# A fused attention and feed-forward layer on one core: the head's products ordered term by term, and six steps in other places

## The chip, the cores and the metric

The kernel runs on one core of a Trainium2 chip. The metric is the device time of one execution in microseconds (us), and a lower time is better. The core's engines have names that are used below: PE is TensorE (matrix products), DVE is VectorE, ACT is ScalarE, POOL is GpSimd, and SP is SyncE, which issues nearly all of the transfers. Each engine works through its own program in order and waits for the others on semaphores.

## The reference

A layer of a network is applied to `x`, 2 sequences of 2048 rows with 1024 features:

```python
qkv = einsum('bsc,cf->bsf', layernorm(x), Wqkv) + bqkv      # q, k, v of 256 features
attn = softmax(q @ k.T * scale, axis=-1)                    # 4 batches by a reshape, d = 256
x = x + (attn @ v) @ Wo + bo
h = relu(layernorm(x) @ up_w) ** 2                          # 2048 wide
shared = h @ down_w
routed = (layernorm(x) @ fc1_w @ expert_w) * sum(top2(gate)) @ fc2_w
x = x + layernorm2(shared + routed) * gamma + beta
```

All of it is in float32.

## The kernel before

**Products.** Each operand of a product is kept as a rounded high half and a low half, which is the operand minus its high half. A product of two operands is three matmuls that add into one bank of PSUM: high by high, high by low, low by high (`mm3`, L2182 to L2184). ACT mostly makes the high half, and DVE (L1191) or POOL (L1960) makes the low half by a subtraction. The names end in `h` and `l`.

**Stages.** The program has four stages, and each engine has its part of all four, written out by hand in one order.

1. *Head.* `e2`, the product of `expert_w` (`et`) and `fc2_w` (`f2`), is accumulated over k = 0 to 3 into seven banks (`lt` 0 to 3, halves `hh` 0 and 1). The eighth, (3,1), is multiplied at the end, since its bank first holds the sums of the first layernorm. Meanwhile DVE takes the statistics of the rows of chunk 0 (`BATCH_NORM`). PE sums them over partitions by two small products, `combine1a` (L2200) and `combine1b` (L2205). DVE then works out mean and root (L1235 to L1266), and the 16 row groups are normalised, those in `NORM_DVE` on DVE (L1273) and the others on ACT (L1017).
2. *Chunks.* In each of 8 chunks of rows the normalised rows `xi` are turned into `xt` (L1285), split into `xh` and `xl` by `slab_hi` and `slab_low`, and multiplied with `w` for q, k and v. DVE takes the statistics of the next chunk and forms sums of feed-forward weights on the way (`pb`, L1300 to L1313). The low half that each chunk needs first is `slab_low(c + 1, 0)`. It is made during chunk c, between the low halves of v.
3. *Attention.* There are 16 pairs of strips, with scores (`kh`, `q`), the row maximum on DVE, the exponential on ACT (`prob`, L937), a transpose, low halves of `pt`, the product with v, and the product with `Wo`. POOL adds the folded bias `bob` to `x` (`xadd`, L2015), DVE adds the attention output (`residual`, L1364) and takes the statistics (`ln2`, L1380 on, with nm at L1386), and POOL normalises (`norm2`, L2006). The folded bias itself is `bv` times `Wo`, four float32 matmuls (L2297) whose result DVE adds to `bo` (L1710).
4. *Feed-forward.* There are four blocks n of 1024 rows. Each has 70 slots of up products and 70 (in the last block 60) of down products. A slot is 12 matmuls, fed by weights that ACT and POOL split (`w_low`: wr0l, wr1l, wr2l) and operands from `x_low`. The function `turnover` starts a slot on an engine. `add_beta` (L2051) adds beta to the residual rows on POOL.

What the change touches: the order of PE's products and sums in the head, the tables `NORM_DVE` and of ACT's staging, `slab_low` on DVE, the place of the bias on PE and DVE, the order of POOL's `xadd` and `norm2` in pairs 7 and 14/15, `ln2(14)`, `x_low(0, 6, ·)`, and the last two calls of `add_beta`.

## Time and profile before

| | before |
|---|---|
| median of 3 runs | 2357.73 us (2353.16 to 2359.95) |
| the profiled execution | 2362.06 us |
| its span | 2360.1 us |
| mean granted clock of PE | 0.996 |
| PE busy | 2310.1 us, 98% of the span |
| DVE busy | 1760.5 us, 75% |
| POOL busy | 1568.0 us, 66% |
| ACT busy | 906.1 us, 38% |

The span is the time from the first to the last instruction in the profile; it differs from the execution's own time by 2.0 us. Busy times are of one execution. In a timeline the bracket behind a row says how long the engine stood idle before it, and which instruction of which engine ended that.

### The profile page before, as it was taken

Reading aid. Unit: us, or ns where it says so; the run is one execution under the profiler, and the core shown is the slowest. Engines: PE = TensorE matmul, PEld = TensorE weight load, DVE = VectorE, ACT = ScalarE, POOL = GpSimd, SP = SyncE. Lnnn points to the kernel's source line nnn. Section 1 sums busy time; section 2 is a strip of 40 time slices with the busy share of each in tenths; the row PEclk is TensorE's granted clock in tenths of the full one; section 3 lists DMA queues with packets and bytes.
Section 4 is the critical chain, followed back from the end, with each engine's and each line's share of the span. In section 5 each row is a group of like instructions: output and inputs, shape, how many; then the busy total and the mean of one; then the engine's idle time right before and its main releaser. Section 6 shows DMA issues by size and latency. Waiting matters only on the chain.

```text
span 2360.1 us, 31294 instructions
## 1 busy us (share of the span) xinstructions
PE 2310.1 (98%) x11224; PEld 1925.1 (82%) x11224; DVE 1760.5 (75%) x2952; ACT 906.1 (38%) x1705; POOL 1568.0 (66%) x1175
## 2 busy tenths in 40 slices
PE   8999999999999999999999999999999999999998
PEld 6888888888888788878887887888887788777786
DVE  5999868778787735854689765579895468979968
ACT  4322243333333344444432443442344443244452
POOL 5556626665665776699567479847649974866762
PEclk9999999999999999999999999999999999999999
DMA  7889656778768633543335345435534433544342
GB/s 260 296 308 317 220 161 187 208 237 297 213 197 234 208 103 94 130 125 115 99 129 180 94 130 126 120 94 161 151 109 122 132 108 112 178 148 129 91 141 86
DMA packets 200137, 386.47 MB, mean 164 GB/s; under 512 B 19120, under 2 KB 78640, under 8 KB 198192
## 3 DMA queue, kind: packets, MB, share of 16 engines
q1 hardware_dynamic: 198832, 382.38, 53.6%
q8 instruction: 90, 1.47, 0.3%
q10 hardware_dynamic: 1152, 2.10, 0.2%
q14 instruction: 63, 0.52, 0.1%
HBM read 260.67 MB, written 90.18 MB: 149 GB/s over the span
## 4 chain that ended last, share of the span: by engine, by line
PE 59%; DVE 15%; POOL 12%; issue 5%; DMA 5%; SPq 2%; ACT 1%; DVEq 0%; POOLq 0%; ACTq 0%
PE ps L2182 20%; PE ps L2184 19%; PE ps L2183 19%; POOL hq L2044 4%; DVE pturn L1337 2%; POOL wr1l L1960 2%; POOL wr2l L1960 2%; POOL wr0l L1960 2%; DMA pland<-pturn 2%; DVE xr L1608 1%; DMA stf<-ups 1%; POOL xr L2051 1%; DVE hq L1517 1%; SPq L640 1%; DVE mx L1320 1%
## 5 line engine op out<-in xcount | busy, mean ns | idle before, releaser
L1960 POOL TENSOR_TENSOR wr2l<-stf,wr2h 128x512 fp32r<-128x512 f32 x183 | 258.6, 1413 | 145.4 <-ACT wr2h L969 145.2
L1960 POOL TENSOR_TENSOR wr1l<-stf,wr1h 128x512 fp32r<-128x512 f32 x183 | 262.5, 1435 | 139.2 <-ACT wr1h L969 139.2
L1960 POOL TENSOR_TENSOR wr0l<-stf,wr0h 128x512 fp32r<-128x512 f32 x184 | 260.7, 1417 | 141.9 <-ACT wr0h L969 141.8
L969 ACT CAST wr0h<-stf 128x512 fp32r<-128x512 f32 x184 | 114.4, 622 | 300.4 <-PE ps L2184 247.9
L969 ACT CAST wr1h<-stf 128x512 fp32r<-128x512 f32 x183 | 113.8, 622 | 299.6 <-PE ps L2184 246.1
L969 ACT CAST wr2h<-stf 128x512 fp32r<-128x512 f32 x183 | 113.9, 622 | 299.1 <-PE ps L2184 244.9
L1960 POOL TENSOR_TENSOR pt<-pland,pt 128x512 fp32r<-128x512 f32 x120 | 153.6, 1317 | 78.7 <-ACT pt L947 78.7
L937 ACT ACTIVATE prob<-ps,nm 128x512 f32<-128x512 f32 x128 | 86.3, 687 | 247.6 <-DVE nm L1328 247.6
L1337 DVE STREAM_TRANSPOSE pturn<-prob 128x512 f32<-128x512 f32 x128 | 131.9, 1089 | 54.0 <-DMA pland<-pturn 51.5
L1191 DVE TENSOR_TENSOR hr1l<-hq,hr1h 128x512 fp32r<-128x512 f32 x78 | 98.7, 1265 | 88.1 <-ACT hr1h L988 88.0
L1191 DVE TENSOR_TENSOR hr2l<-hq,hr2h 128x512 fp32r<-128x512 f32 x78 | 98.1, 1258 | 87.3 <-ACT hr2h L988 87.3
L1191 DVE TENSOR_TENSOR hr0l<-hq,hr0h 128x512 fp32r<-128x512 f32 x78 | 96.0, 1231 | 87.3 <-ACT hr0h L988 87.3
L2182 PE MATMUL ps<-pt,vh 128*128 128x256 f32 x512 | 145.8, 285 | 5.3 <-DVE pt L1191 5.2
L2183 PE MATMUL ps<-pt,vh 128*128 128x256 f32 x512 | 145.6, 284 | 0.0
L2184 PE MATMUL ps<-pt,vl 128*128 128x256 f32 x512 | 145.5, 284 | 0.0
L2044 POOL TENSOR_TENSOR hq<-hq,hq 128x512 f32<-128x512 f32 x90 | 140.6, 1562 | 0.0
L1960 POOL TENSOR_TENSOR xl<-xt,xh 128x512 fp32r<-128x512 f32 x54 | 71.9, 1343 | 72.2 <-ACT xh L927 72.1
L2006 POOL TENSOR_SCALAR x<-x,nm,rst 128x1024 f32<-128x1024 f32 x28 | 33.6, 1211 | 119.8 <-DVE rst L1205 119.8
L2182 PE MATMUL ps<-xh,wh 128*128 128x512 f32 x256 | 102.1, 399 | 3.6 <-DVE xl L1191 3.6
L2182 PEld LDWEIGHTS ps<-pt,vh 128*128 128x128 f32 x512 | 98.9, 193 | 7.2 <-issue 6.0
L2182 PE MATMUL ps<-kh,q 128*128 128x512 f32 x256 | 101.1, 395 | 2.7 <-ACT prob L937 2.7
L2183 PE MATMUL ps<-kl,q 128*128 128x512 f32 x256 | 100.5, 393 | 0.0
(490 smaller groups left out, 7746.5 us busy)
## 6 DMA issues: line engine op xcount, KB each, us to landing
stf<-ups SPq DMA_DIRECT2D x160, 256.0 KB, 3.2
stf<-downs SPq DMA_DIRECT2D x160, 256.0 KB, 2.9
pland<-pturn SPq DMA_DIRECT2D x120, 256.0 KB, 4.7
stf<-in_upw_dram SPq DMA_DIRECT2D x120, 256.0 KB, 2.7
stf<-in_down_dram SPq DMA_DIRECT2D x88, 256.0 KB, 2.7
x<-in_x_dram SPq DMA_DIRECT2D x32, 512.0 KB, 6.6
x1d<-x SPq DMA_DIRECT2D x32, 512.0 KB, 5.7
xi<-in_xc_dram SPq DMA_DIRECT2D x7, 2048.0 KB, 9.0
```

Source lines behind the costliest of these rows:

```text
L640: eng.dma_start(land(g)[:, 512 * i + 32 * n * h:512 * i + 32 * n * (h + 1)], turned(g)[32 * i:32 * i + 32, :].rearrange("p (k s) -> p k s" ...
L937: eng.activation(prob[:, 512 * kb:512 * kb + 512], ps[:, kb, :], ACT.Exp, bias=nm[:, 0:1], scale=1.0 / 16, accum_out=rs[:, kb:kb + 1]).the ...
L969: eng.copy(hi, src).then_inc(*a_w.up(K))
L1191: eng.tensor_tensor(lo, src, hi.bitcast(F32), ALU.subtract).then_inc(*done)
L1320: eng.reduce_max(mx[:, kb:kb + 1], ps[:, kb, :], AX.X).then_inc(*v_mx.up((g, kb)))
L1337: eng.transpose(turned(g)[:, :].rearrange("p (k s b) -> p s k b", k=4, b=32)[:, 4 * kb:4 * kb + 4], prob[:, 512 * kb:512 * kb + 512].rearr ...
L1960: eng.tensor_tensor(lo, src, hi.bitcast(F32), ALU.subtract).then_inc(*done)
L2006: eng.tensor_scalar(x2n[C][i][:, :], x1t[i][:, :], nm2[:, i:i + 1], rst2[:, i:i + 1], ALU.add, ALU.mult).then_inc(*g_x2.up(g))
L2044: eng.tensor_tensor(hq[o][:, c, :], hq[a][:, c, :], hq[b][:, c, :], op).then_inc(*g_hs.up((n, name, c)))
L2182: eng.matmul(o, ah, bh, start=first, stop=False)
L2183: eng.matmul(o, ah, bl, start=False, stop=False)
L2184: return eng.matmul(o, al, bh, start=False, stop=last)
```

## The change

**Head.** For k = 2 and 3 PE multiplies one term over all banks before the next term (`e2_term`). The first sum of statistics stands after 8 of these matmuls and the second after 7 more. `NORM_DVE` has ten groups in place of six. POOL makes the low half of `et` 3 ahead of that of `f2` 3. ACT splits `w` (2,0) before it normalises, takes out `e2` banks for `lt` 0 ahead of `slab_hi(0, 0)`, and splits `w` (1,1) before those for `lt` 1.

**Chunks.** `slab_low(c + 1, 0)` stands ahead of the turns of slabs 2 and 3.

**Folded bias.** Its four matmuls move from between chunk 7's v and the scores of strip 1 to between the scores of strips 2 and 3, and DVE's addition moves with them, to after the first low halves of `pt`.

**Pair 7.** POOL's `xadd(6, 0)` stands ahead of `norm2(5)`.

**Pairs 14 and 15.** `ln2(14)` works on one column at a time (two by turns), and its root has other steps (22 small instructions in place of 11 after the aggregate). POOL's `norm2(14)` comes ahead of `xadd(15)`, whose halves move into slots 0 and 1, and SP stores both results in slot 0.

**Feed-forward.** `x_low(0, 6, ·)` goes one slot later; the last betas go from slots 50 and 53 of up to slots 33 and 37 of down.

```diff
-        NORM_DVE = (1, 3, 6, 9, 12, 15)
+        NORM_DVE = (1, 3, 5, 7, 8, 9, 11, 12, 14, 15)
...
-            for k in STG[:12]:
+            for k in STG[:13]:
                 stage_hi(k)
             norm_rows(0, [g for g in range(16) if g not in NORM_DVE])
-            stage_hi(STG[12])
+            e2_evac(0)
             slab_hi(0, 0)
-            e2_evac(0)
+            stage_hi(STG[13])
+            e2_evac(1)
             slab_hi(0, 1)
-            e2_evac(1)
-            for k in STG[13:15]:
-                stage_hi(k)
+            stage_hi(STG[14])
...
                     low(v_parts(c, t), a_v[c, t], v_v.up((c, t)))
+                    if c < 7 and t == 1:
+                        slab_low(c + 1, 0)
                     if c < 7 and t < 2:
                         turn1(c + 1, 2 * t)
                         turn1(c + 1, 2 * t + 1)
-                    if c < 7 and t == 1:
-                        slab_low(c + 1, 0)
...
-            ln2(14, *range(15))
+            ln2(14)
...
                 if C == 7:
+                    xadd(C - 1, 0)
                     norm2(C - 2, 0)
                     norm2(C - 2, 1)
-                if C < 15 and C != 8:
+                    xadd(C - 1, 1)
+                elif C < 15 and C != 8:
                     xadd(C - 1)
...
-            xadd(15)
+            norm2(14, 0)
+            norm2(14, 1)
...
-                        if s in (1, 2):
-                            norm2(14, s - 1)
+                        if s < 2:
+                            xadd(15, s)
...
-                        if fin and s in (50, 53):
-                            add_beta(n, (s - 50) // 3, xrl[(s - 50) // 3])
...
+                        if s in (33, 37):
+                            add_beta(n, s // 37, xrl[s // 37])
...
+            e2_term(2, eth, f2h, 0)
+            w.wait_ge(*stg_lo(("et", 2)))
+            e2_term(2, etl, f2h, 0)
+            combine1a(0)
+            w.wait_ge(*stg_lo(("f2", 2, 0)))
+            e2_term(2, eth, f2l, 0)
+            w.wait_ge(*a_stg["f2", 2, 1])
+            e2_term(2, eth, f2h, 1)
+            combine1b(0)
...
                     scores(even)
                     if C >= 2:
                         outputs(C - 2)
+                    else:
+                        folded_bias()
                     scores(odd)
```

How the rows move on PE in the head, at k = 2, where `mv,quad` is `combine1a` and `dm,quad` is `combine1b`. Before:

```order
L2223 MATMUL ps<-f2h,eth 128x512 x4
L2223 MATMUL ps<-f2h,etl 128x512 x4
L2223 MATMUL ps<-f2l,eth 128x512 x4
L2200 MATMUL ps<-mv_54,quad 128x32
L2182 MATMUL ps<-f2h,eth 128x512
L2183 MATMUL ps<-f2l,eth 128x512
L2184 MATMUL ps<-f2h,etl 128x512
L2182 MATMUL ps<-f2h,eth 128x512
L2183 MATMUL ps<-f2l,eth 128x512
L2184 MATMUL ps<-f2h,etl 128x512
L2182 MATMUL ps<-f2h,eth 128x512
L2183 MATMUL ps<-f2l,eth 128x512
L2184 MATMUL ps<-f2h,etl 128x512
L2205 MATMUL ps<-dm_55,quad 128x16
```

After:

```order
L2260 MATMUL ps<-f2h,eth 128x512 x4
L2260 MATMUL ps<-f2h,etl 128x512 x4
L2235 MATMUL ps<-mv_54,quad 128x32
L2260 MATMUL ps<-f2l,eth 128x512 x4
L2260 MATMUL ps<-f2h,eth 128x512 x3
L2240 MATMUL ps<-dm_55,quad 128x16
L2260 MATMUL ps<-f2h,etl 128x512 x3
L2260 MATMUL ps<-f2l,eth 128x512 x3
L2260 MATMUL ps<-f2h,eth 128x512 x7
L2260 MATMUL ps<-f2h,etl 128x512 x7
```

The first sum stands four matmuls earlier and the second, counted from it, two.

How they move on DVE between chunks 0 and 1, where `xt<-xi` is a turn, `xl<-xt,xh` the chunk's first low half and `vl` a low half of v. Before:

```order
L1285 STREAM_TRANSPOSE xt_98<-xi_97 128x512
L1285 STREAM_TRANSPOSE xt_99<-xi_97 128x512
L1191 TENSOR_TENSOR vl<-ps,vh 128x2x128
L1285 STREAM_TRANSPOSE xt_100<-xi_97 128x512
L1285 STREAM_TRANSPOSE xt_101<-xi_97 128x512
L1191 TENSOR_TENSOR xl<-xt_98,xh 128x512
L1191 TENSOR_TENSOR vl<-ps,vh 128x2x128 x2
```

After:

```order
L1286 STREAM_TRANSPOSE xt_98<-xi_97 128x512
L1286 STREAM_TRANSPOSE xt_99<-xi_97 128x512
L1192 TENSOR_TENSOR vl<-ps,vh 128x2x128
L1192 TENSOR_TENSOR xl<-xt_98,xh 128x512
L1286 STREAM_TRANSPOSE xt_100<-xi_97 128x512
L1286 STREAM_TRANSPOSE xt_101<-xi_97 128x512
L1192 TENSOR_TENSOR vl<-ps,vh 128x2x128 x2
```

The low half has moved ahead of two turns; the same piece stands at all seven chunk boundaries.

How they move on POOL where the feed-forward stage begins, where `x2e` is `norm2(14)`, `x<-x,bob` is `xadd(15)`, and `wr` are the weights of slots 0 to 5. Before:

```order
L1960 TENSOR_TENSOR wr0l<-stf_217,wr0h 128x512
L1960 TENSOR_TENSOR wr1l<-stf_218,wr1h 128x512
L1960 TENSOR_TENSOR wr2l<-stf_219,wr2h 128x512
L2015 TENSOR_TENSOR x_126<-x_126,bob 128x512 x2
L2015 TENSOR_TENSOR x_127<-x_127,bob 128x512 x2
L1960 TENSOR_TENSOR wr0l<-stf_217,wr0h 128x512
L1960 TENSOR_TENSOR wr1l<-stf_218,wr1h 128x512
L2006 TENSOR_SCALAR x2e_137<-x_128,nm_70,rst_68 128x1024
L1960 TENSOR_TENSOR wr2l<-stf_219,wr2h 128x512
L2006 TENSOR_SCALAR x2e_138<-x_129,nm_70,rst_68 128x1024
```

After:

```order
L1992 TENSOR_TENSOR wr0l<-stf_217,wr0h 128x512
L1992 TENSOR_TENSOR wr1l<-stf_218,wr1h 128x512
L1992 TENSOR_TENSOR wr2l<-stf_219,wr2h 128x512
L2038 TENSOR_SCALAR x2e_137<-x_128,nm_70,rst_68 128x1024
L2038 TENSOR_SCALAR x2e_138<-x_129,nm_70,rst_68 128x1024
L1992 TENSOR_TENSOR wr0l<-stf_217,wr0h 128x512
L2047 TENSOR_TENSOR x_126<-x_126,bob 128x512 x2
L1992 TENSOR_TENSOR wr1l<-stf_218,wr1h 128x512
L2047 TENSOR_TENSOR x_127<-x_127,bob 128x512 x2
L1992 TENSOR_TENSOR wr2l<-stf_219,wr2h 128x512
```

Both normalisations have moved ahead of four additions, and the additions stand between the low halves of slots 3, 4 and 5.

## Rows read from the trace of the kernel before

**Rows 1.** Waits of PE over the span: total us, times, longest us.

```profile
PE ps L2200 <- DVE mv L1220: 1.3, 2, 0.7
```

**Rows 2.** Timeline of the head: start us, us, engine, line, tile [idle before].

```profile
21.70 0.30 PE L2200 MATMUL ps<-mv,quad 128*128 128x32 f32 x2
...
24.09 0.29 PE L2205 MATMUL ps<-dm,quad 128*128 128x16 f32 x2
...
25.48 0.51 PE L2182 MATMUL ps<-f2h,eth 128*128 128x512 f32 x1 [1.10 <-POOL etl L1960]
...
36.19 0.79 PE L2182 MATMUL ps<-xh,wh 128*128 128x512 f32 x1 [2.92 <-DVE xl L1191]
...
39.34 0.40 PE L2183 MATMUL ps<-xl,wh 128*128 128x512 f32 x1
...
19.80 0.64 DVE L1220 BATCH_NORM_AGGREGATE mv<-st 128x2 f32<-128x6 f32 x8
...
27.07 2.02 DVE L1273 TENSOR_SCALAR xi<-xi,nmean,rst 128x256 f32<-128x256 f32 x6
...
34.14 1.99 DVE L1191 TENSOR_TENSOR xl<-xt,xh 128x512 fp32r<-128x512 f32 x1 [0.69 <-ACT xh L927]
...
27.19 5.03 ACT L1017 ACTIVATE xi<-xi,nb,rst 128x256 f32<-128x256 f32 x10 [4.20 <-DVE nb L1266]
```

**Rows 3.** Timeline: chunk 1's first matmul; chunk 3's low half; chunks 4 and 5's statistics.

```profile
72.53 0.50 PE L2182 MATMUL ps<-xh,wh 128*128 128x512 f32 x1 [0.69 <-DVE xl L1191]
...
138.67 0.69 DVE L1191 TENSOR_TENSOR xl<-xt,xh 128x512 fp32r<-128x512 f32 x1 [1.91 <-ACT xh L927]
...
184.56 1.17 DVE L1220 BATCH_NORM_AGGREGATE mv<-st 128x2 f32<-128x6 f32 x16
...
185.94 0.30 PE L2200 MATMUL ps<-mv,quad 128*128 128x32 f32 x2
...
217.78 1.17 DVE L1220 BATCH_NORM_AGGREGATE mv<-st 128x2 f32<-128x6 f32 x16
...
219.74 0.30 PE L2200 MATMUL ps<-mv,quad 128*128 128x32 f32 x2
```

**Rows 4.** Windows low half to aggregate, chunks 3 to 6, their sum.

```profile
sum 49.60, PE 48.47 PEld 40.42 DVE 49.21 ACT 11.98 POOL 42.69; mean PE 12.12 PEld 10.10 DVE 12.30 ACT 2.99 POOL 10.67
```

**Rows 5.** Timeline of PE around the folded bias and strip 3's scores.

```profile
310.39 3.60 PE L2297 MATMUL ps<-wos,bvb 128*128 128x512 f32 x8
...
313.42 0.79 PE L2182 MATMUL ps<-kh,q 128*128 128x512 f32 x1
...
332.67 0.64 PE L2182 MATMUL ps<-kh,q 128*128 128x512 f32 x1 [1.98 <-ACT prob L937]
...
336.42 0.40 PE L2182 MATMUL ps<-kh,q 128*128 128x512 f32 x1
```

**Rows 6.** Timeline of pair 7's start on POOL, DVE and PE.

```profile
524.66 4.98 POOL L2015 TENSOR_TENSOR x<-x,bob 128x512 f32<-128x512 f32 x4
...
528.40 0.75 DVE L1364 SCALAR_TENSOR_TENSOR x<-ps,rinv,x 128x512 f32<-128x512 f32 x1 [6.21 <-POOL x L2015]
...
530.33 0.36 PE L2182 MATMUL ps<-pt,vh 128*128 128x256 f32 x1 [3.46 <-DVE pt L1191]
```

**Rows 7.** Timeline of the FFN's start on DVE, POOL and PE.

```profile
769.30 12.50 DVE L1386 TENSOR_SCALAR nm<-mv 128x2 f32<-128x2 f32 x1
...
774.23 5.05 POOL L2015 TENSOR_TENSOR x<-x,bob 128x512 f32<-128x512 f32 x4
...
784.15 1.20 POOL L2006 TENSOR_SCALAR x2e<-x,nm,rst 128x1024 f32<-128x1024 f32 x1 [2.37 <-DVE rst L1205]
...
786.38 0.47 PE L2182 MATMUL ps<-xop01h,wr1h 128*128 128x512 f32 x1 [1.97 <-DVE x L1364]
```

**Rows 8.** Timeline of PE in the first and in the last FFN block.

```profile
832.78 0.50 PE L2182 MATMUL ps<-xop02h,wr1h 128*128 128x512 f32 x1 [1.28 <-POOL wr1l L1960]
...
2154.96 0.50 PE L2182 MATMUL ps<-wr1h,hr0h 128*128 128x512 f32 x1 [0.96 <-DVE hq L1490]
```

More of the change, by code:

```diff
@@ L265, in layer @@
         e2_bank = {(lt, hh): 2 * lt + hh if lt < 3 else 7 - hh for lt in range(4) for hh in range(2)}
-        p_e2 = ev("p_e2", [k for k in e2_bank])
+        p_e2 = ev("p_e2", [(lt, hh) for hh in range(2) for lt in range(4)])
         p_stat = ev("p_stat", [(c, x) for c in range(8) for x in "ab"])
@@ L356, in layer @@
         g_chain = Chain(sem("g_chain"))
-        g_stg = ev("g_stg", [k for k in STG if k not in STG_DVE])
+        g_stg = ev("g_stg", sorted([k for k in STG if k not in STG_DVE],
+                                   key=lambda k: STG.index(k) - 2 * (k == ("et", 3))))
         g_slab = ev("g_slab", [k for k in SLABS if k not in SLAB_DVE])
@@ L369, in layer @@
         g_xb = ev("g_xb", [(n, t) for n in range(NBK)
-                           for t in (range(8) if n < NBK - 1 else (0, 1, 4, 5, 6, 7, 2, 3))])
+                           for t in (range(8) if n < NBK - 1 else (4, 5, 6, 7, 2, 3, 0, 1))])
         g_mid = ev("g_mid", [(t, hh) for t in (2, 3) for hh in range(2)])
@@ L1765, in _ @@
                     maxima(odd)
-                    ln2(C - 2, *range(15))
+                    ln2_wide(C - 2, *range(15))
                     turns(odd)
@@ L1779, in _ @@
                     at_low(C - 1, 1)
-                    ln2(C - 2, *range(15))
+                    ln2_wide(C - 2, *range(15))
                 elif C == 15:
@@ L1792, in _ @@
                     at_low(C - 1, 1)
-                    ln2(C - 2, *range(15))
+                    ln2_wide(C - 2, *range(15))
                 else:
@@ L1798, in _ @@
                     maxima(odd)
-                    ln2(C - 2, *range(15))
+                    ln2_wide(C - 2, *range(15))
                     turns(odd)
@@ L2007, in norm2, with xadd @@
                                   ).then_inc(*g_x2.up(g))
-            def xadd(C):
-                for i in range(2):
+            def xadd(C, *rows_of):
+                for i in rows_of or range(2):
                     w.wait_ge(*d_x[i][2 * C + i])
@@ L2120, in _ @@
                             norm2(15, s - 3)
-                        if 14 <= s < 18:
-                            x_low(0, 6, s - 14)
+                        if 15 <= s < 19:
+                            x_low(0, 6, s - 15)
                         if s in (19, 21, 23, 25):
@@ L2215, in _ @@
                 e2_part(0, lt, 1)
[L2216 to L2237 removed]
+            w.wait_ge(*stg_lo(("et", 1)))
@@ new lines, in _, with e2_term @@
+            for hh in range(2):
+                w.wait_ge(*stg_lo(("f2", 1, hh)))
+                for lt in range(4 - hh):
+                    e2_part(1, lt, hh)
+            def e2_term(k, a, b, hh, last=False):
+                for lt in range(4 - hh):
+                    ins = eng.matmul(ps[:, e2_bank[lt, hh], :], a[:, k, 128 * lt:128 * lt + 128],
+                                     b[:, k, 512 * hh:512 * hh + 512], start=False, stop=last)
+                    if last:
+                        ins.then_inc(*p_e2.up((lt, hh)))
@@ L2238, in _ @@
+            w.wait_ge(*a_stg["f2", 3])
+            w.wait_ge(*a_stg["et", 3])
+            for hh in range(2):
+                e2_term(3, eth, f2h, hh)
+            w.wait_ge(*stg_lo(("et", 3)))
+            for hh in range(2):
+                e2_term(3, etl, f2h, hh)
+            w.wait_ge(*stg_lo(("f2", 3)))
+            for hh in range(2):
+                e2_term(3, eth, f2l, hh, True)
             w.wait_ge(*v_nb[0])
@@ L2288, in _ @@
                             ins.then_inc(*p_v.up((c, t, j)))
-                    if c == 7 and t == 1:
-                        w.wait_ge(*d_wo[0])
-                        w.wait_ge(*v_bvb[0])
-                        w.wait_ge(*a_e2[3, 0])
-                        w.wait_ge(*v_v[6, 2])
-                        w.wait_ge(*v_rst[7])
-                        for hh in range(2):
-                            for d in range(2):
-                                ins = eng.matmul(ps[:, 6 + hh, :], bvb[:, d, :], wos[:, d, 512 * hh:512 * hh + 512],
-                                                 start=d == 0, stop=d == 1)
-                        ins.then_inc(*p_bob.up(0))
                     if c == 7 and t <= 1:
@@ L2382, in outputs, with folded_bias @@
                     wo_unit(C, u)
+            def folded_bias():
+                w.wait_ge(*d_wo[0])
+                w.wait_ge(*v_bvb[0])
+                w.wait_ge(*a_e2[3, 0])
+                w.wait_ge(*v_v[7, 3])
+                w.wait_ge(*v_rst[7])
+                for hh in range(2):
+                    for d in range(2):
+                        ins = eng.matmul(ps[:, 6 + hh, :], bvb[:, d, :], wos[:, d, 512 * hh:512 * hh + 512],
+                                         start=d == 0, stop=d == 1)
+                ins.then_inc(*p_bob.up(0))
             for C in range(1, 16):
@@ L2403, in _ @@
                         outputs(C - 2)
+                    else:
+                        folded_bias()
                     scores(odd)
```

76 lines of the change are left out of this document (44 added, 32 removed).

## The prediction, made before the changed kernel ran

> **What bounds the kernel now.** I read the page first: PE is busy for 2310.1 of 2360.1 us, so the change can only work on the 50 us in which PE idles, and on stretches in which PE's clock is low. Then I read the list of what PE waited for, of which one row is shown [rows 1], and looked up each wait in the timeline, with what the releasing engine did before. The waits near the edits are 2.92 us at the end of the head [rows 2], 0.69 us at chunk 1 [rows 3], two of up to 0.7 us on the statistics of later chunks [rows 1], 1.98 us in strip 3's scores [rows 5], 3.46 us in pair 7 [rows 6], 1.97 us as the feed-forward stage begins [rows 7], and 1.28 and 0.96 us in it [rows 8].
>
> A wait can cost more than its length. Nine matmuls and a small product lie between the head's two sums, 2.39 us with the small one's 0.3 taken off: 0.23 us for a matmul. Behind the 2.92 us wait seven matmuls took from 36.19 to 39.34, 0.45 each [rows 2]. Behind the 1.98 us wait nine took 3.75, 0.42 each [rows 5]. The records there are longer (0.79 and 0.64 us), as at the lower of the clock's two levels. So the two waits cost another 1.5 and 1.7 us. Behind the 1.28 us wait the row is 0.50 us long, the full clock's length [rows 8], so the point at which a wait starts to cost double lies between 1.3 and 2.0 us.
>
> **The head.** The aggregate ends at 20.44, but PE starts its first sum at 21.70, behind twelve matmuls [rows 2]. After the change it stands behind eight, four times 0.23 earlier: 20.8. The second sum then follows after seven matmuls and not nine, another 0.46 earlier, and the 0.3 us that the sum itself takes is unchanged: 24.09 - 0.9 - 0.5 = 22.7. DVE's root starts with it, so the normalising starts at 27.07 - 1.4 = 25.7. Six groups took DVE 2.02 us (0.34 each) and ten took ACT 5.03 us (0.50 each), so ACT ended last, at 32.2 [rows 2]. With ten on DVE (3.4 us) and six on ACT (3.0 us) both end near 29.1, 3.1 us earlier. The first low half ended at 36.13; it now ends near 33.0 if POOL stretches it as before, and near 31.8 if it takes the 0.69 us of the same operation at 138.67 [rows 2, 3].
> PE ended the head at 36.19 - 2.92 = 33.27. The wait of 1.10 us for POOL's low half of `et` 3 goes, since that half is made first and is asked for last [rows 2]: 32.2. A wait of 0 to 0.8 us is left, too short to lower the clock by the rows above. I take chunk 0 to start at 32.7. Before, its start at the full pace would have been 39.34 - 7 x 0.23 = 37.7. The gain is 5.0 us. Upper bound: no wait, 5.5. Lower bound: the low clock stays (1.5) and the first low half is another 1.0 late, 2.5.
>
> **The chunk's first low half.** It goes ahead of two turns. What it waits for is ACT's high half: at 138.67 DVE had been idle for 1.91 us for it [rows 3], after both turns. If the turns now stand behind it, they no longer fill this idle time. The ACT half is made only after v's third strip, whatever DVE does. So DVE has the two turns (1.22 us together by the start of the next row) still to do when it used to be through with them. From there to the aggregate nothing is idle: over chunks 3 to 6 DVE was busy for 49.21 of 49.60 us [rows 4]. So the aggregate comes 1.22 us later against PE. Chunk 1 is the exception: its half was ready before the second pair of turns, and PE's wait of 0.69 us goes [rows 3]. PE waited for the aggregate in chunks 3 and 6 already [rows 1], and each of these waits grows by 1.22. In chunk 4 PE's sum at 185.94 came 0.21 us after the aggregate (184.56 + 1.17 = 185.73), a new wait of 1.0; in chunk 5 219.74 stands against 218.95, a new wait of 0.4 [rows 3]. Sum: 2 x 1.22 + 1.0 + 0.4 - 0.7 = 3.2 us lost. Bounds: a gain of 0.7 if DVE has cover that I don't see; a loss of 6.6 if the waits of 0.7 + 1.2 = 1.9 us in chunks 3 and 6 lower the clock (2 x 1.7).
>
> **The folded bias.** The four matmuls take PE 3.03 us (310.39 to 313.42) [rows 5], and they cost that in both places. Moved, they make everything from strip 1's scores on 3.0 us earlier and then stand just where PE waited 1.98 us for strip 2's exponential. That exponential's maxima follow PE's scores, so it is 3.0 us earlier too. PE works on the bias for 3.0 us where it would have idled for 2.0, so the wait and the slow matmuls behind it go: 1.98 + 1.7 = 3.7 us gained. The bias is fp32 and keeps PE busy. DVE's addition (covered by PE's 3 us) moves behind the low halves of strip 0 and is needed only by POOL's `xadd`, some pairs later. Bounds: 0, if the wait for the exponential only moves, to 3.8.
>
> **Pair 7.** DVE's residual, on which the low half and so PE's 3.46 us wait hang, started at 528.40, and its `x` was ready after two of four additions, 524.66 + 2.5 = 527.15 [rows 6]. So something else released it, and the transfer that stores the rows of pair 5 lands about then. I take 0. Upper bound 3.5 (2.1 us from the two normalisations ahead, and the slow pace), lower bound -0.3.
>
> **Pairs 14 and 15.** DVE's `nm` of pair 14, a 128x2 operation that otherwise takes 0.17 us, took 12.50 us, until 781.8. POOL worked without a pause to just then: its four additions ran from 774.23 to 779.28 and two low halves followed. Then came the root, `norm2(14)` at 784.15, the residual and PE, 1.97 us late at 786.38 [rows 7], and the slow pace, again 1.7. With `norm2(14)` in front POOL stops at 774.2 and waits for the root. So DVE is let in by then at the latest, the root ends about 776.6 (2.4 us from nm to root, as 781.8 to 784.15), and `norm2(14)` ends by 779.0. The additions follow, two of them by 782.7, and the residual that PE needs at 784.4 is done at 783.5. That saves 3.7 us. Against it: the low halves of slots 4 and 5 have four additions and a slot's weights in front, and that of slot 5 comes 0.7 us late. I take 3.0. Bounds 1.7 (the wait stays under a lowered clock's threshold but does not go) and 3.7.
> The page "SBUF — State Buffer" of the Trainium skill, section "SBUF: two separate sides", says that DVE and GpSimd share a port pair which one of them holds for its whole instruction while the other is fully blocked. By that rule `nm` would have got in after one POOL instruction, some 1.3 us, and all of the new small operations would do so too; the trace has it outside for ten. By the rule alone the old order would lose nothing here and this term would be 0; the 12.50 us row decides for 3.0.
>
> **The feed-forward stage.** `x_low(0, 6, ·)` goes one slot later, away from the low half for which PE waited 1.28 us at 832.78 [rows 8]: I take 0.7 (0 to 1.28). The last betas leave the end of the last up stage, where DVE had no idle time and PE waited 0.96 us for it at 2154.96 [rows 8]; they go to down slots where DVE has some. I take 1.0 (from 1.0, to -1.0 if the same wait turns up there).
>
> **Sum.** 5.0 - 3.2 + 3.7 + 0 + 3.0 + 0.7 + 1.0 = 10.2 us gained. The profiled execution would go from 2362.06 to 2351.9, which is 0.43%. The profiled execution lies 4.3 us above the median of the runs, 2357.73, so against the median the forecast is 2347.5 us. Measurements of this kernel tell about 0.3% from no change, 7.1 us.
>
> **The rivals.**
> 1. *Chunk waits lower the clock.* The two waits of 1.9 us are just between the 1.3 us that cost nothing more and the 1.98 that did. Then 3.4 us more go: 10.2 - 3.4 = 6.8 gained, 2350.9. For it: every number is within 0.1 us of the 1.98 us wait. Against it: PE was never pausing before it. Chance 0.19.
> 2. *Only head, bias and chunks count.* The waits of the attention and feed-forward stages come from other causes and turn up a few us later: 5.0 - 3.2 + 3.7 = 5.5 gained, 2352.2. For it: DVE is loaded there, and what PE gains it can lose at the next operand; for pair 14 it holds if the 12.5 us had another cause than POOL's unbroken work. By the rule of the skill's page above it would be so there. Chance 0.16.
> 3. *The head gains half*, as weights of chunk 0 are late on POOL: 10.2 - 2.5 = 7.7, 2350.0. Chance 0.12.
> 4. *Slower.* Moving the low half delays DVE in every chunk by more than the turns: if its slack before the statistics is used up in chunks 2 to 6 and each wait lowers the clock, each chunk loses 1.22 + 1.7 + up to 1.3 for high halves that come late in turn, 4.2 x 5 = 21 us against 14 gained elsewhere: 7 us slower, 2364.9. It decides from 2.7 us a chunk. Against it: DVE's other idle time of 1.91 us per chunk [rows 3] takes up what is late before the next low half. Chance 0.04.
>
> **How the numbers follow.** The forecast of 2347.5 has 0.49. Faster by over 0.3%: 0.49, 0.12 of rival 3, and a small part of rival 1, 0.04: 0.65. Within 0.3%: the rest of 1, and 2: 0.31. Slower: 0.04. The upper end of the range leaves out rival 4 and the worst of 2: 2355. The lower end adds what the upper bounds allow for the chunks or for pair 7 (3.5) and the rest (3): 2341.
>
> **What the profile would show.** Head: the first sum at 20.8, the second at 22.7, first matmul of chunk 0 at 32.2 to 33.0, with 0.23 us pace. Chunks: no wait at chunk 1, statistics waits of 1.9, 1.0, 0.4 and 1.9 us in chunks 3 to 6. Bias: no wait at strip 3. Pair 7: still about 3.5 us. Pair 14: POOL idle from 774 (less the shift) to the root, and no 12.5 us operation. I am wrong if DVE's aggregates are not late, if a wait moves from strip 2's exponential to the bias or behind it, or if the 12.5 us blocking comes back on another small operation.

## The result

The changed kernel takes 2344.43 us, the median of 4 runs (2344.20 to 2347.34), against 2357.46 us before: a ratio of 0.9945, with a 95% interval of 0.9933 to 0.9957, so 13.0 us or 0.55% faster. The forecast was 2347.5 us with a range from 2341 to 2355. The profiled execution went from 2362.06 to 2344.41 us.

The page of the changed kernel, part 1. PE works 6.5 us less, and its idle time fell from 50 to 38.9 us.

```profile
PE 2303.6 (98%) x11224; PEld 1919.9 (82%) x11224; DVE 1747.8 (75%) x2965; ACT 903.4 (39%) x1701; POOL 1571.4 (67%) x1175
```

To see where the time came from, I laid the two PE timelines side by side, matmul by matmul. The offset is the start of a matmul before minus its start after. Where it steps, time was gained or lost. The steps add up to the 17.6 us between the two profiled executions, which is 4.6 us more than between the medians, so not all of it is the change's.

| place | predicted | step in the offset |
|---|---|---|
| head, to chunk 0 at full pace | +5.0 | +7.4 |
| chunks | -3.2 | +0.4 (+1.0 at chunk 1, -0.6 later) |
| folded bias | +3.7 | +3.9 |
| pair 7 | 0 | +1.9 |
| a new wait at 584.4 (0.95 us) and a shorter one at 742.7 | - | -0.9 |
| pairs 14 and 15 at the stage's start | +3.0 | +3.6 |
| up slots of block 0, before and at `x_low(0, 6)` | +0.7 | -1.2 |
| rest of the feed-forward stage, no part of the change | - | +2.4 |
| last betas | +1.0 | +0.1 |

The head after the change, in the timeline of PE, DVE and ACT, to be read beside [rows 2]:

```profile
18.13 0.30 PE L2235 MATMUL ps<-mv,quad 128*128 128x32 f32 x2
...
19.98 0.29 PE L2240 MATMUL ps<-dm,quad 128*128 128x16 f32 x2
...
29.38 0.50 PE L2217 MATMUL ps<-xh,wh 128*128 128x512 f32 x1 [0.15 <-DVE xl L1192]
...
17.04 0.65 DVE L1221 BATCH_NORM_AGGREGATE mv<-st 128x2 f32<-128x6 f32 x8
...
22.96 3.32 DVE L1274 TENSOR_SCALAR xi<-xi,nmean,rst 128x256 f32<-128x256 f32 x10
...
27.71 1.61 DVE L1192 TENSOR_TENSOR xl<-xt,xh 128x512 fp32r<-128x512 f32 x1 [0.69 <-ACT xh L929]
...
23.08 3.07 ACT L1019 ACTIVATE xi<-xi,nb,rst 128x256 f32<-128x256 f32 x6 [1.40 <-DVE nb L1267]
```

The sums stand at 18.1 and 20.0, DVE's ten groups and ACT's six end together at 26.2, and PE waits 0.15 us before chunk 0, and 0.68 us for a low half of `w` at 31.72, with no slow matmuls behind either. But the aggregate itself ends 2.75 us earlier than in [rows 2], at 17.69, which no edit on DVE explains. It goes with the first transfers: in the trace of before PE waited 0.82 and 1.10 us for halves of `f2` at k = 1 and 2, and here not at all. Experiment 3, with the old head and no such waits, has the end of the aggregate at 17.31.

The boundary to chunk 3, beside [rows 3]: DVE's low half, the two turns, the weight sum, the aggregate, and PE's sum.

```profile
130.32 0.69 DVE L1192 TENSOR_TENSOR xl<-xt,xh 128x512 fp32r<-128x512 f32 x1 [3.12 <-ACT xh L929]
...
130.93 1.30 DVE L1286 STREAM_TRANSPOSE xt<-xi 128x512 f32<-128x512 f32 x2
...
132.15 0.38 DVE L1301 TENSOR_TENSOR pb<-pb 128x256 f32<-128x256 f32 x1
...
142.52 1.17 DVE L1221 BATCH_NORM_AGGREGATE mv<-st 128x2 f32<-128x6 f32 x16
...
143.74 0.41 PE L2235 MATMUL ps<-mv,quad 128*128 128x32 f32 x2 [0.74 <-DVE mv L1221]
```

DVE is idle 1.21 us longer before the low half, just as forecast (3.12 for 1.91). Yet from the start of the low half to that of the aggregate it takes 12.20 us, and before it took 150.79 - 138.67 = 12.12. The two turns cost nothing: the weight sum `pb` behind them takes 0.38 us. These rows of before show what it took there, and what POOL did then:

```profile
139.28 1.53 DVE L1300 TENSOR_TENSOR pb<-pb 128x256 f32<-128x256 f32 x1
...
139.24 1.29 POOL L1960 TENSOR_TENSOR xl<-xt,xh 128x512 fp32r<-128x512 f32 x1 [13.33 <-ACT xh L927]
```

The sum began at 139.28 beside POOL's low half of slab 1, which ran from 139.24 to 140.53, and ended 0.28 us behind it. The turns have taken the place in which DVE was held.

The folded bias and the matmul behind it, for [rows 5]. PE doesn't wait there, and 0.39 us records follow.

```profile
319.30 3.59 PE L2433 MATMUL ps<-wos,bvb 128*128 128x512 f32 x8
...
322.33 0.79 PE L2217 MATMUL ps<-kh,q 128*128 128x512 f32 x1
```

Pair 7, for [rows 6], with SP's issue of the store: the residual starts 5.6 us behind it, and the trace names the store as what released it. PE still waits 3.03 us, but this time the next record is 0.28 us long: no low clock behind a wait of 3 us.

```profile
511.04 2.24 SPq L660 DMA_DIRECT2D x1d<-x  x2
...
516.62 0.75 DVE L1365 SCALAR_TENSOR_TENSOR x<-ps,rinv,x 128x512 f32<-128x512 f32 x1 [4.04 <-DMA x1d<-x]
...
517.29 2.48 DVE L1192 TENSOR_TENSOR pt<-pland,pt 128x512 fp32r<-128x512 f32 x2
...
518.24 0.35 PE L2217 MATMUL ps<-pt,vh 128*128 128x256 f32 x1 [3.03 <-DVE pt L1192]
...
518.79 0.28 PE L2218 MATMUL ps<-pt,vh 128*128 128x256 f32 x1
```

The start of the feed-forward stage, for [rows 7]: none of the 22 small operations is held, and POOL goes from its low halves to `norm2(14)` without idling, the root being there at 759.5.

```profile
756.51 0.23 DVE L1406 TENSOR_SCALAR nm<-mv 128x1 f32<-128x1 f32 x2
...
759.05 0.46 DVE L1418 TENSOR_SCALAR rst<-tmp,rst 128x1 f32<-128x1 f32 x2
...
760.26 1.29 POOL L1992 TENSOR_TENSOR wr2l<-stf,wr2h 128x512 fp32r<-128x512 f32 x1
...
761.54 2.38 POOL L2038 TENSOR_SCALAR x2e<-x,nm,rst 128x1024 f32<-128x1024 f32 x2
...
768.18 0.75 DVE L1365 SCALAR_TENSOR_TENSOR x<-ps,rinv,x 128x512 f32<-128x512 f32 x1 [8.68 <-POOL x L2047]
```

The two places of [rows 8]: the wait before `x_low`'s slots is 1.36 us in place of 1.28, now for the operand, and 0.96 us before the down slots went, while this wait at down slot 42 is new.

```profile
822.42 0.50 PE L2217 MATMUL ps<-xopAh,wr2h 128*128 128x512 f32 x1 [1.36 <-POOL xopAl L1992]
...
2254.16 0.47 PE L2217 MATMUL ps<-wr1h,hr0h 128*128 128x512 f32 x1 [0.62 <-DVE hr0l L1192]
```

### The profile page after: what moved, and what is told of

Its sections match the earlier page's. It is cut to its first block, busy times and chain, and to the rows that moved or that the text cites. A ratio compares the mean times of both kernels' runs of the same rounds, so it can differ in the third digit from the quotient of the medians.

```text
span 2342.5 us, 31302 instructions
## 1 busy us (share of the span) xinstructions
PE 2303.6 (98%) x11224; PEld 1919.9 (82%) x11224; DVE 1747.8 (75%) x2965; ACT 903.4 (39%) x1701; POOL 1571.4 (67%) x1175
## 4 chain that ended last, share of the span: by engine, by line
PE 56%; DVE 17%; POOL 11%; DMA 8%; issue 4%; SPq 2%; ACT 1%; DVEq 0%; POOLq 0%; ACTq 0%
PE ps L2217 18%; PE ps L2219 18%; PE ps L2218 18%; DVE pturn L1338 5%; DMA pland<-pturn 4%; POOL hq L2076 3%; SPq L641 2%; POOL wr1l L1992 2%; POOL wr0l L1992 2%; POOL wr2l L1992 2%; DVE x L1365 1%; DVE mx L1321 1%; POOL xr L2083 1%; DMA stf<-ups 1%; DMA stf<-downs 1%
```

## The experiments

Each kernel is the changed one with the edit shown. Times are medians of 5 to 11 runs. The single runs of one kernel spread over 4 to 8 us. A ratio is to the kernel before, run again beside each experiment, and its interval is some 3 us to either side. Only the intervals of experiments 2 and 3 lie clear of the changed kernel's (0.9933 to 0.9957), and that of 4 nearly does; what the other edits cost is read from the traces.

**1. The low half behind the turns again.**

```diff
-                    if c < 7 and t == 1:
-                        slab_low(c + 1, 0)
                     if c < 7 and t < 2:
                         turn1(c + 1, 2 * t)
                         turn1(c + 1, 2 * t + 1)
+                    if c < 7 and t == 1:
+                        slab_low(c + 1, 0)
```

> The changed kernel with one part undone: the chunk's first low half stands behind the turns of slabs 2 and 3 again. Theory A (the turns stand where DVE would otherwise be held off the shared port by POOL's low half of slab 1): the weight sum behind the low half takes 1.2 to 1.5 us again in place of 0.38 to 0.41, the span from low half to aggregate in chunk 3 stays 12.1 to 12.2 us, PE's waits on the statistics stay 0.6 to 0.8 us in chunks 3 and 6, and PE waits about 0.7 us at the start of chunk 1. Time 0.3 to 0.9 us above the changed kernel's 2344.4: 2345. Theory B (the turns cost DVE 1.22 us in each chunk, as I predicted, and something else hid it): the statistics waits shrink to nothing and the time falls by about 3 us, 2341.

2345.08 us, ratio 0.9953 (0.9940 to 0.9965). The wait at chunk 1 is back with 0.69 us, the weight sum takes 1.53 us again in chunk 3, from low half to aggregate it is 12.12 us, and the statistics wait in chunk 6 is 0.67. At the end of the chunks it is 0.4 us behind the changed kernel. Theory A; this part of the change is worth 0.4 us.

**2. The weight sum ahead of the turns.**

```diff
                     if c < 7 and t == 1:
                         slab_low(c + 1, 0)
+                        prep(c, 8 + t)
                     if c < 7 and t < 2:
                         turn1(c + 1, 2 * t)
                         turn1(c + 1, 2 * t + 1)
...
-                    prep(c, 8 + t)
+                    if c == 7 or t != 1:
+                        prep(c, 8 + t)
```

> The changed kernel with the weight sums' step of that place moved too: low half, then the weight sum, then the two turns. Theory A: the weight sum stands next to POOL's low half of slab 1 again and takes 1.2 to 1.5 us, and the turns behind it cost their full 1.22 us, so the span from low half to aggregate in chunk 3 grows from 12.2 to 13.4 us and PE's statistics waits to 1.9 us in chunks 3 and 6, with about 1.0 and 0.4 us in chunks 4 and 5: 3.5 us slower than the changed kernel or more (2348, and 2351 if waits of 1.9 us lower the clock). Theory B (order among DVE's operations makes no difference there): no change, 2344.4.

2352.39 us, ratio 0.9982 (0.9973 to 0.9990), 8 us slower than the changed kernel. Chunk 3 on DVE and PE:

```profile
131.39 0.69 DVE L1192 TENSOR_TENSOR xl<-xt,xh 128x512 fp32r<-128x512 f32 x1 [3.12 <-ACT xh L929]
...
132.00 1.53 DVE L1301 TENSOR_TENSOR pb<-pb 128x256 f32<-128x256 f32 x1
...
134.33 1.29 DVE L1286 STREAM_TRANSPOSE xt<-xi 128x512 f32<-128x512 f32 x2
...
145.56 1.17 DVE L1221 BATCH_NORM_AGGREGATE mv<-st 128x2 f32<-128x6 f32 x16
...
146.78 0.41 PE L2237 MATMUL ps<-mv,quad 128*128 128x32 f32 x2 [2.71 <-DVE mv L1221]
```

The same operations, with `pb` directly behind the low half: it is held again, 1.53 us, and the turns now cost their full time. From low half to aggregate it is 14.17 us, and PE waits 2.71 us in chunks 3 and 6. That is more than the 1.9 us expected, since a later weight sum is held too (1.48 us for 0.62). Theory A: the loss of my forecast was real for this order, not for the one that was made. Behind the first wait of 2.71 us PE stays at full pace, behind the second it falls to the low clock for seven matmuls.

**3. All of the head undone** (the tables, the staging orders, and PE's order as before).

```diff
-            e2_term(2, eth, f2h, 0)
-            e2_term(2, etl, f2h, 0)
-            combine1a(0)
...
+                    combine1a(0)
+                    for lt in range(3):
+                        e2_part(2, lt, 1)
+                    combine1b(0)
...
-        NORM_DVE = (1, 3, 5, 7, 8, 9, 11, 12, 14, 15)
+        NORM_DVE = (1, 3, 6, 9, 12, 15)
```

> The changed kernel with all of the head's part undone. Theory A: of the 7.2 us by which chunk 0 starts earlier in the changed kernel's trace, about 5 are the change's and about 2.5 are landings of the first transfers, which differ between executions. Then chunk 0 gets going about 5 us later than in the changed kernel once its first f2 landings are taken off, with a wait of about 3 us before the first matmul of chunk 0 and the slow pace behind it, and the time is 2349.5. Theory B: all 7.2 us are the change's (its order on ACT and POOL frees staging buffers earlier): 2351.6, and the waits on f2 of 0.8 and 1.1 us at k = 1 and 2 are there in this trace too.

2351.37 us, ratio 0.9977 (0.9968 to 0.9985), 6.9 us slower. PE's first matmul of chunk 0:

```profile
33.72 0.79 PE L2217 MATMUL ps<-xh,wh 128*128 128x512 f32 x1 [3.32 <-DVE xl L1192]
```

Here nothing waits for `f2`, and once the pace is back, PE is 6.2 us behind the changed kernel and stays so through all chunks. So the head is worth 6.2 us, and the other 1.2 of the 7.4 in the table were the landings of the first transfers in that one execution. Theory A, with a size 1.2 us larger than expected.

**4. The folded bias in chunk 7 again.**

```diff
-                    else:
-                        folded_bias()
...
+                    if c == 7 and t == 1:
+                        for hh in range(2):
+                            for d in range(2):
+                                ins = eng.matmul(ps[:, 6 + hh, :], bvb[:, d, :], wos[:, d, 512 * hh:512 * hh + 512],
+                                                 start=d == 0, stop=d == 1)
+                        ins.then_inc(*p_bob.up(0))
```

> The changed kernel with the folded bias back between chunk 7's v and strip 1's scores, and DVE's addition with it. Theory A: PE waits about 2.0 us for strip 2's exponential, the pace behind it is 0.42 us a matmul for about nine, and the time is 3.7 us above the changed kernel's: 2348.1. Theory B (the wait was due to what came before and has moved with the earlier head): less than 1 us, 2345.

2349.89 us, ratio 0.9967 (0.9956 to 0.9978), 5.5 us slower. The wait is back, as long as before:

```profile
326.58 0.50 PE L2218 MATMUL ps<-kh,q 128*128 128x512 f32 x1 [1.97 <-ACT prob L939]
```

But this record is 0.50 us long where [rows 5] has 0.64, and no slow matmuls follow. At 328 us of the changed kernel's time this trace is 4.0 us late; 1.7 of that it already had from waits on `f2` at the start. So the part is worth 2.3 us where the clock holds, and 3.9 where it falls. Theory A in the wait, not in the pace. The median says more, 5.5, within the spread of the runs.

**5. POOL's order in pair 7 undone.**

```diff
                 if C == 7:
-                    xadd(C - 1, 0)
                     norm2(C - 2, 0)
                     norm2(C - 2, 1)
-                    xadd(C - 1, 1)
-                elif C < 15 and C != 8:
+                if C < 15 and C != 8:
                     xadd(C - 1)
```

> The changed kernel with POOL's two normalisations of pair 5 ahead of both halves of the addition for pair 6 again. Theory A (the residual on which PE waits in pair 7 is released by the store of pair 5's rows, which SP issues behind four loads of the transposed probabilities): the residual starts 6 us after that store's issue as before, PE waits 3.0 to 4.3 us with the slow pace behind the longer ones, and the time is within 1 us of the changed kernel's 2344.4. Theory B (POOL's order releases it): the residual starts 1.3 to 2.5 us later against the store's issue, 2347.

2345.70 us, ratio 0.9945 (0.9931 to 0.9959): no difference, theory A. The residual starts 5.2 us behind the store's issue, and PE waits 3.45 us, as in [rows 6], with the slow pace behind it as there. With the new order the wait is 3.00 to 3.03 us in the traces of the changed kernel and of experiments 8 and 11, with no slow pace behind it, and 4.20 to 4.35 with the slow pace in 1, 2, 3, 4, 7 and 10. In all nine POOL begins its own low halves of `pt` 2.2 to 2.4 us after PE has stopped. Where the wait is short, DVE's low half begins 0.11 to 0.47 us ahead of POOL's, and PE goes on 0.85 to 1.22 us after that start; where it is long, DVE's begins from 0.01 us ahead to 0.56 behind, and PE goes on 1.41 to 1.97 us after. What is ahead of DVE's low half is the residual, so its release decides whether DVE or POOL is first. I take that to be the switch, but it wasn't tried alone. So the 1.9 us in the table are a lucky execution's and not a gain of the order.

**6. SP's store ahead of the loads.**

```diff
                     xload(C - 1)
-                    shuffle(odd)
                     store1(C - 2)
+                    shuffle(odd)
```

> The changed kernel with one thing more: in pair 7 SP issues the stores of pair 5's rows ahead of the four loads of transposed probabilities, that is as soon as the rows of pair 6 are asked for, some 9 us earlier. Theory A (the store's landing is what PE waits for in pair 7): the residual starts when POOL's first normalisation of pair 5 is done, 2.5 us or more earlier, PE's wait of 3.0 to 4.3 us shrinks to 1.5 us at most and the slow pace goes; about 1 us is given back in the next pairs: 2341 to 2342. Theory B (the store is only the last of several that come together): under 0.7 us, 2344.

2349.83 us, ratio 0.9958 (0.9944 to 0.9971): no gain, and neither theory. By the medians it is 5.4 us slower than the changed kernel, but the intervals overlap, and the profiled execution, 4.0 us behind after pair 7, took 2345.11 in all. First the issue of the probabilities in the changed kernel, between 505 and 520 us, then here DVE and PE:

```profile
pland<-pturn SPq DMA_DIRECT2D x4, 256.0 KB, 4.5
...
514.36 0.75 DVE L1365 SCALAR_TENSOR_TENSOR x<-ps,rinv,x 128x512 f32<-128x512 f32 x1 [1.45 <-POOL x L2038]
...
520.05 0.69 DVE L1192 TENSOR_TENSOR pt<-pland,pt 128x512 fp32r<-128x512 f32 x1 [4.94 <-ACT pt L949]
...
520.89 0.55 PE L2217 MATMUL ps<-pt,vh 128*128 128x256 f32 x1 [5.32 <-DVE pt L1192]
```

The residual is released 2.3 us earlier, by POOL, so the store did hold it. But the transposed probabilities now land after 8.1 us in place of 4.5, and PE waits 5.32 us for their low half.

**7. Pair 14's root in its old form, POOL in the new order.**

```diff
-            ln2(14)
+            ln2_wide(14, *range(15))
```

> The changed kernel with pair 14's root in its old form, 11 operations on two columns in place of 22 on one, while POOL keeps the new order. Theory A (operations of the old form are held off while POOL works without a pause, those of the new form are not): nm is held until POOL stops for the root behind the low half of slot 2's weights, some 5 us, the root ends 2.4 us behind that, and PE waits about 1 us more at slots 4 to 6 or finds them just in time: 2345 to 2347. Theory B (POOL's order alone took the 12.5 us away): nm takes 0.2 us, 2344.4.

2349.15 us, ratio 0.9958 (0.9945 to 0.9971). DVE and POOL:

```profile
760.98 5.03 DVE L1387 TENSOR_SCALAR nm<-mv 128x2 f32<-128x2 f32 x1
...
764.69 1.29 POOL L1992 TENSOR_TENSOR wr2l<-stf,wr2h 128x512 fp32r<-128x512 f32 x1
...
768.35 2.38 POOL L2038 TENSOR_SCALAR x2e<-x,nm,rst 128x1024 f32<-128x1024 f32 x2 [2.37 <-DVE rst L1206]
```

`nm` is held for 5.03 us, to 766.01, and POOL's last low half ended at 765.98. PE waits 0.71 and 1.28 us at slots 5 and 7, where the changed kernel waits 0 and 0.34, and loses 2.0 us here. Theory A. (The rest of the 4.7 us between the medians is the longer wait of pair 7, which this trace has too, or chance. The old form has 13 operations behind the aggregate, `nm`, `var` and 11 for the root; the 11 named ahead of the prediction and in the expectation are the root's alone.)

**8. The new form, POOL in the old order.**

```diff
-            norm2(14, 0)
-            norm2(14, 1)
+            xadd(15)
...
-                        if s < 2:
-                            xadd(15, s)
+                        if s in (1, 2):
+                            norm2(14, s - 1)
```

> The changed kernel with POOL's (and SP's) old order around pairs 14 and 15, but pair 14's root in its new form of 22 operations on one column. Theory A (the form of the operations was the cause of the 12.5 us): the root ends within 3 us of the aggregate though POOL never pauses, POOL normalises pair 14 in slots 1 and 2 without a wait, and PE's wait at slot 4 is under 0.7 us: 2344.4 to 2345.4. Theory B (the order was the cause): one of the small operations is held for about 12 us, PE waits 2 us at slot 4 and goes slow behind it, 2348.

2345.97 us, ratio 0.9954 (0.9938 to 0.9970). DVE, POOL and PE:

```profile
755.63 0.22 DVE L1405 TENSOR_SCALAR nm<-mv 128x1 f32<-128x1 f32 x2
...
758.17 0.46 DVE L1417 TENSOR_SCALAR rst<-tmp,rst 128x1 f32<-128x1 f32 x2
...
756.88 1.31 POOL L1991 TENSOR_TENSOR wr0l<-stf,wr0h 128x512 fp32r<-128x512 f32 x1
...
760.62 5.04 POOL L2046 TENSOR_TENSOR x<-x,bob 128x512 f32<-128x512 f32 x4
...
780.45 0.50 PE L2215 MATMUL ps<-xop01h,wr1h 128*128 128x512 f32 x1 [1.51 <-POOL wr1l L1991]
```

POOL works without a pause from 751.89 to 773.05, and none of the 22 operations is held. There is no wait at slot 4, and 1.51 us at slot 7, where the changed kernel waits 0.34 us: 1.2 us are lost against it from slot 0 to there. Theory A: the form of the operations takes the 12.5 us away, and POOL's order is worth about 1 us. What in the form counts, one element in place of two or an input without a step between its elements, was not tried.

**9. The last k loads behind q** (with the edit of experiment 6).

```diff
                     shuffle(odd)
-                    for kb in (2, 3):
-                        load_k(kb)
...
                     qload(C + 2)
+                if C == 7:
+                    for kb in (2, 3):
+                        load_k(kb)
```

> The kernel of the store ahead of the loads, and in pair 7 the last four loads of the second sequence's k (2 MB) behind the load of q, so that neither they nor the store stand beside the transposed probabilities. Theory A (pair 7 is bound by the transfers: moving the store alone only let the probabilities land 3.6 us later, 8.1 us from issue to landing in place of 4.5): the probabilities land within 5.5 us, PE's wait in pair 7 shrinks from 5.3 us to under 2.5, the slow pace goes, and the time is 2340 to 2342. Theory B (what delays the probabilities are the 4 MB issued before them, k's first half, x and the store): the wait stays over 4 us, 2347 or more.

2343.81 us, ratio 0.9943 (0.9929 to 0.9956). The DMA issues between 505 and 520 us (KB each, median us to landing), then DVE:

```profile
pland<-pturn SPq DMA_DIRECT2D x4, 256.0 KB, 6.8
...
514.43 0.75 DVE L1366 SCALAR_TENSOR_TENSOR x<-ps,rinv,x 128x512 f32<-128x512 f32 x1 [1.45 <-POOL x L2039]
...
517.53 2.65 DVE L1193 TENSOR_TENSOR pt<-pland,pt 128x512 fp32r<-128x512 f32 x2 [2.35 <-ACT pt L950]
```

The probabilities land after 6.8 us, 1.3 earlier than in 6, and PE waits 3.05 us for them, then 0.81 us for k. The residual is no longer what ends last. The time is that of the changed kernel, and the numbers lie between the two theories.

**10. `x_low(0, 6)` one slot earlier, the last betas in the up stage.**

```diff
-                        if 15 <= s < 19:
-                            x_low(0, 6, s - 15)
+                        if 14 <= s < 18:
+                            x_low(0, 6, s - 14)
...
+                        if fin and s in (50, 53):
+                            add_beta(n, (s - 50) // 3, xrl[(s - 50) // 3])
...
-                        if s in (33, 37):
-                            add_beta(n, s // 37, xrl[s // 37])
```

> The changed kernel with two of its parts undone, which lie far apart: x_low(0, 6) one slot earlier again, and the last betas in up slots 50 and 53 again. From the two traces, theory A: the operand's move only changed which operand PE waits for (1.28 us before, 1.36 after), 0.0 to 0.5 us; the betas' move took away 1.6 us of waits at the start of the last down stage and gave 0.4 to 0.9 us of waits near down slots 33 and 37, so undone they cost 0.7 to 1.2 us. Time 2344.4 + 0.7 = 2345. Theory B (as I predicted): both parts were gains, 0.7 and 1.0: 2346.1.

2346.82 us, ratio 0.9958 (0.9945 to 0.9972).

```profile
819.33 0.50 PE L2217 MATMUL ps<-xop02h,wr1h 128*128 128x512 f32 x1 [1.32 <-POOL wr1l L1992]
...
2138.23 0.50 PE L2217 MATMUL ps<-wr1h,hr0h 128*128 128x512 f32 x1 [0.95 <-DVE hq L1523]
```

The wait of 1.32 us is back and that of 1.36 at the operand gone; over this stretch the trace gets 0.45 us ahead of the changed kernel, and those of 1, 5, 6 and 7, which keep the part, get 0.9 ahead. The waits for the betas cost 2.2 us up to 2139, and 2.1 of it comes back in the 120 us that follow, where the changed kernel waits. Both parts are worth nothing that can be told from the scatter: within 0.5 us of nothing for the operand, as theory A has it, and 0.1 for the betas, less than either theory.

**11. Only the split of the normalising undone.**

```diff
-        NORM_DVE = (1, 3, 5, 7, 8, 9, 11, 12, 14, 15)
+        NORM_DVE = (1, 3, 6, 9, 12, 15)
```

> The changed kernel with six of the sixteen row groups of chunk 0 normalised on DVE and ten on ACT again, all else of the head as changed. Theory A (the chain of statistics, root, normalising, turn and first low half ends last, PE's own products do not): ACT ends 5.0 us after the root and not 3.3, PE waits 1.9 us more before chunk 0's first matmul, 2.0 in all, and 1.5 more if the clock falls: 2346.3 to 2347.9. Theory B (the head is then bound by PE's products or by the low halves of w on POOL, which come later too): under 1 us, 2345.

2347.55 us, ratio 0.9962 (0.9949 to 0.9976).

```profile
24.02 5.04 ACT L1019 ACTIVATE xi<-xi,nb,rst 128x256 f32<-128x256 f32 x10 [2.08 <-DVE nb L1267]
...
31.73 0.50 PE L2217 MATMUL ps<-xh,wh 128*128 128x512 f32 x1 [1.57 <-DVE xl L1192]
```

ACT takes 5.04 us again, and PE waits 1.57 us before chunk 0, 1.4 more than the changed kernel, where theory A had 1.9 more. Through the chunks it is 2.0 us behind, but 0.9 of that it had at 26 us already, ahead of the normalising: its clock first rose at 10.5 us, and that of the changed kernel at 8.5. So the split is worth about 1 us, a sixth of the head's gain, and the places of the sums and of `et` 3 are the rest, with the pace that holds.

**12. All k loads behind the probabilities.**

```diff
-                if C == 7:
-                    for kb in (0, 1):
-                        load_k(kb)
...
                     store1(C - 2)
                     shuffle(odd)
+                    for kb in (0, 1):
+                        load_k(kb)
```

> The kernel of the late k loads, with k's first 2 MB too behind the transposed probabilities, so that ahead of them in pair 7 stand only x and the store (2 MB in place of 4). Theory A (each load's landing is set by the bytes issued before it in this stretch, in which the transfers move some 330 to 400 GB/s): x and the store land about 5 us earlier, the probabilities within 5 us of their issue and not 6.8, PE's wait of 3.05 us in pair 7 shrinks to 0.5 to 1.5, and what is not given back before the scores of strip 16, which need k's first blocks some 13 us after their issue (up to 1 us), is gained: 2341.5 to 2343. Theory B (the wait only moves to k at the scores of strip 16): 3 us or more there, 2345 or slower.

2350.24 us, ratio 0.9957 (0.9944 to 0.9971). The trace is 5.7 us behind the changed kernel's after pair 7. The DMA issues, then PE:

```profile
pland<-pturn SPq DMA_DIRECT2D x4, 256.0 KB, 4.6
...
518.56 0.77 PE L2217 MATMUL ps<-kh,q 128*128 128x512 f32 x1 [5.60 <-issue]
...
523.82 0.41 PE L2217 MATMUL ps<-pt,vh 128*128 128x256 f32 x1
```

The probabilities land after 4.6 us and the wait for them is gone: PE goes from the scores straight to `pt`. But the scores of strip 16, which PE takes first, now wait 5.60 us (the trace gives "issue", and what is late is the load of k, issued from 511.5 on and landing after 7.6 to 8.7 us), and eleven matmuls or more at the low clock follow. Theory B.

## Why the prediction was right, and where not

**Total.** The direction and the size hold, 13.0 us against 10.2, but that is in part luck, since errors of both signs offset each other: the chunks come out 3.6 us better and the head 1.2 better, and the two parts of the feed-forward stage gain over 1 us less. The medians' 13.0 us has an interval of about 10 to 16.

**The head: right in mechanism, 1.2 us too small.** Each step is there: the sums, the root, the split that ends level, no wait for `et` 3, and full pace. The term measured 6.2 us (experiment 3) for the 5.0 forecast: 4.3 for 3.5 in the start of chunk 0 (33.72 against 29.38), and 1.9 for 1.5 in the slow pace behind it. The rows that I worked from had late `f2` landings, and there PE's first sum stood 1.3 us behind the aggregate, where it stands 2.0 behind without them (19.31 against 17.31), so the new order had more to take away.

**The chunks: wrong.** The step that failed is "From there to the aggregate nothing is idle: over chunks 3 to 6 DVE was busy for 49.21 of 49.60 us [rows 4]. So the aggregate comes 1.22 us later against PE." Busy was not the same as working: 1.15 of the 1.53 us of `pb` were a hold beside POOL's low half, and a turn, with one input, runs there at its full pace. Experiments 1 and 2 show it with the same operations in three orders: 12.12, 12.20 and 14.17 us. The page "SBUF — State Buffer" of the Trainium skill, section "SBUF: two separate sides", has just this case: a DVE operation with two inputs in SBUF is blocked by a GpSimd operation that reads SBUF. The traces agree, with 1.53 us in place of 0.38. I had weighed that rule for pair 14 and not here. Rival 1, whose base was this delay, falls with it.

**The bias: right,** 3.9 us in the two traces compared for 3.7. Of it 1.6 hangs on the clock, which fell before and did not in experiment 4.

**Pair 7: right for the reason given.** The store released the residual. That the wait can't be mended by moving one transfer is new: in experiments 6, 9 and 12 what ended last was in turn the probabilities, these again, and k.

**Pairs 14 and 15: right in size (3.6 for 3.0), half right in cause.** I gave POOL's new order as what lets DVE in. It would have cost about 2 us more (experiment 7), for DVE got in only when POOL stopped, as I had worked out. What helps is that the new operations on one column are not held at all (experiment 8). The rule of the skill's page, as I read it, one instruction of POOL per hold and all small operations under it, fits neither: `nm` was held through ten instructions in the kernel before and four in experiment 7, and the one-column operations through none. The same section of the page names as blocked only DVE operations in a two-port mode or with two inputs in SBUF, which I had left out; no run here shows in which mode an operation ran. Nor is it a rule that POOL must pause. In the changed kernel the two-column form of pair 13 stood beside POOL's four low halves of `pt`, which ran from 733.62 to 738.66 without a pause:

```profile
736.82 0.62 DVE L1387 TENSOR_SCALAR nm<-mv 128x2 f32<-128x2 f32 x1
...
737.36 1.33 DVE L1389 TENSOR_SCALAR var<-mv 128x2 f32<-128x2 f32 x1
```

`nm` ended at 737.44, 0.03 us behind the third of them, with the fourth already begun at 737.36, and `var` was held through that fourth alone. Why the holds before slot 0 lasted for ten and four instructions stays open.

**The feed-forward stage: two terms mis-sized.** `x_low` measured within 0.5 us of nothing for 0.7, and the betas 0.1 for 1.0: in both, the work put elsewhere made waits of about the same length there. That was the lower case that I had named for the betas alone.

**The clock.** That "the point at which a wait starts to cost double lies between 1.3 and 2.0 us" is wrong as a single point. Over all traces no wait up to 1.79 us lowered the clock, every one from 3.3 us on did, and between 1.97 and 3.05 us both happened: 1.97 with and without, 2.16 without, 2.71 with and without, 2.92 with, 3.00 to 3.05 without.

## What to carry to other kernels

An engine that is busy for 99% of a stretch may still be held in it. Compare each operation's time with the shortest of its kind before calling its neighbours costly. If one is held, put work there that the other engine doesn't hold. Before crediting a gain to a stretch, look whether the wait there is the same in several executions: pair 7's was 3.0 or 4.2 us, and the slow pace came with the longer one. A wait removed from a part that is bound by transfers can turn up at the next transfer, as it did in experiments 6, 9 and 12.

## What the runs showed of the hardware

- A DVE operation on two SBUF inputs beside POOL's subtraction took 1.53 us in place of 0.38. Two transposes at the same place took 1.30, as elsewhere.
- A `TENSOR_SCALAR` on 128x2 elements was held for 12.50 and 5.03 us, until POOL paused; elsewhere the same form got in between two POOL instructions with no pause between them (0.62 us). Twenty-two on 128x1 elements ran in 3.0 us beside POOL at work.
- PE's granted clock fell behind waits from 1.97 us on, but not behind each: the waits of 3.00 to 3.05 us in pair 7 left it up in four traces.
- In pair 7, four loads of 256 KB took 4.5 to 8.1 us from issue to landing, depending on what had been issued ahead of them.
